# Products that nobody reads, at a block's end and beside 24 maxima

## The chip, the cores and the metric

The kernel runs on one core of a Trainium2 chip (trn2). Its time is the device time of one execution, in microseconds. It is written at the level of engines: each of the five (TensorE or PE, VectorE or DVE, ScalarE or ACT, GpSimd or POOL, SyncE or SP) has its own program, and semaphores order them.

## The reference

Two layers of a transformer over 2 batches of 1024 tokens with 256 features, in float32. Each layer is attention, an addition and layer norm, then a mixture of experts, an addition and layer norm. The change lies around the second layer's attention, which isn't causal:

```
qkv = x @ Wqkv + bqkv
q, k, v = jnp.split(qkv, [D, D + KV], axis=-1)
q = q.reshape(b, s, H, HD)                                # H = 16 heads of 16
k = jnp.tile(k.reshape(b, s, G, HD), (1, 1, H // G, 1))   # G = 4
v = jnp.tile(v.reshape(b, s, G, HD), (1, 1, H // G, 1))
scores = jnp.einsum('bqhd,bkhd->bhqk', q, k) / HD
prob = jax.nn.softmax(scores, axis=-1)
out = jnp.einsum('bhqk,bkhd->bqhd', prob, v).reshape(b, s, D)
return out @ Wout + bout
```

## The kernel before

The program is a row of blocks; at the end of a block all engines meet at a barrier. Three blocks matter here.

Block `p1` (`in_turn`) does batch 1's layer norm and its projections to queries, keys and values: 16 transposes, ACT's square root, 16 transposes back, and eight tasks of products (`("pj", m, c)`, six products of 128x512 each by `mm3`, lines 86 to 88) and transposes of the values. Beside these tasks ACT and VectorE also prepare weights for later blocks (`Projection`, `RouterWeights`). Its eight PSUM banks form a ring; a bank's reader raises `emptied`.

Block `a1` (`grouped_attention`) is the second attention. It works in 16 units (batch, four heads of each group, 512 queries), each of 16 steps. For the softmax's maximum it computes the scores twice. First with queries on the partitions: `maxima` issues two products of 48 rows by 512 columns (line 1697) into one of two slots of PSUM (`mx_ps`), and VectorE reduces the slot's 1024 columns to one negated maximum per query (line 1830, semaphore `mx_taken`). TensorE may fill a slot again when its reduction is done. The 48 rows are 16 features of queries, split in a high and a low part; heads lie at partition 0 or at 64, in turn. After the 16 maxima of a unit `turn` transposes them (line 1738), ACT copies them (line 1789), and SP sends them to the queries' tile as a 49th row (line 1668). Then keys stand on the partitions: `scores` (line 1712, one product of 49 rows), ACT's exponential (line 1811), and `values` (line 1725). The maxima run a unit and a half ahead of the scores. So 24 of them, the list `FIRST`, come ahead of the loop, with the first turn behind the 16th:

```
for u, i in FIRST:
    bank = room(ring.a_max())
    for half in range(2):
        maxima(u, i, half, bank)
    if (u, i) == (0, STEPS - 1):
        turn(-1, False, True, room(ring.a_turn(-1, False, True)))
```

The loop over units and steps follows. In each step stand, in TensorE's order, the values of an earlier step, then by turns two products of a maximum and two of scores. In unit 0 the values begin with step 4. Scores write three banks, `st_ps`, unused until then. After the attention, block `f1` has the second mixture of experts.

Of the kernel before, what the change touches and what calls it, by code (L numbers as in the profile page):

```python
# [13 lines left out]
P = 128  # L14
# [4 lines left out]
CH = 512  # L19
# [588 lines left out]
FORE = [("nf", s) for s in range(4)]  # L608
BACK = [("nb", s) for s in range(4)]
# [931 lines left out]
def grouped_attention(nc, tag, counters, queries, sides, ks, vs, z, ident, psum, rear):  # L1541
# [14 lines left out]
    with Phase(nc, tag, psum) as am:  # L1556
# [10 lines left out]
        st_ps = am.ps([P, 3, CH])  # L1567
# [112 lines left out]
        @block.tensor  # L1680
        def _(pe):
            ring = Slots()

            def room(at):
                for sem, n in at[1] or ():
                    pe.wait_ge(sem, n)
                return at[0]

            def maxima(u, i, half, bank):
                b, j, c = UNITS[u]  # L1690
                q, g = head_of(i)
                p0 = (g // 2) * HALFP
                if i == 0 and half == 0:
                    pe.wait_ge(q_in[u % QSLOT], (u // QSLOT + 1) * 192)
                    if j == 0 and c == 0:
                        pe.wait_ge(sides[b].k_in, sides[b].K_LOADS)
                m = pe.matmul(mx_ps[:, bank, half, :], qq[p0:p0 + ROWS, u % QSLOT, g % 2, q * P:(q + 1) * P],  # L1697
                              ks[b][p0:p0 + ROWS, g % 2, half * CH:(half + 1) * CH], start=True, stop=True)
                if half == 1:
                    m.then_inc(mx_ready, 1)  # L1700

            def scores(u, i, k):
                b, j, c = UNITS[u]
                n = u * 2 * STEPS + 2 * i + k
                kt, g = i // 2, (1 - i % 2) * 2 + k
                p0 = (g // 2) * HALFP
                if i == 0 and k == 0:
                    pe.wait_ge(m_in[u % QSLOT], (u // QSLOT + 1) * 64)
                if n >= 3:

                    pe.wait_ge(exp_done, n - 2)
                pe.matmul(st_ps[:, n % 3, :], ks[b][p0:p0 + ROWS + 1, g % 2, kt * P:(kt + 1) * P],  # L1712
                          qq[p0:p0 + ROWS + 1, u % QSLOT, g % 2, :], start=True, stop=True).then_inc(st_ready, 1)

            def values(n, half):
                u, kt = n // NK, n % NK
                b, j, c = UNITS[u]
                x = slice(half * CH // 2, (half + 1) * CH // 2)
                if half == 0:
                    pe.wait_ge(exp_done, (n + 1) * G1)  # L1720
                if kt == 0 and half == 0 and u >= 1:

                    pe.wait_ge(zt_done, u)
                for g in range(G1):
                    m = pe.matmul(acc_ps[g * W:(g + 1) * W, x], vs[b][:, kt, g, :], pt[:, n % SLOTS, g, x],  # L1725
                                  start=kt + half == 0, stop=kt + half == NK, tile_position=(0, g * W))
                if half == 1:
                    m.then_inc(pv_done, 1)

            def turn(u, with_z, with_m, bank):  # L1730
                if with_z:
                    pe.wait_ge(zt_done, u)
                    for q in range(NQ):
                        m = pe.transpose(mx_ps[:, bank, 0, q * P:(q + 1) * P], zt[:, q * P:(q + 1) * P], ident[:])
                    m.then_inc(z_turned, 1)
                if with_m:
                    pe.wait_ge(mx_taken, (u + 2) * STEPS)
                    pe.transpose(mx_ps[0:G1 * NQ, bank, 1, 0:P], negm[:, (u + 1) % 2, :], ident[:]).then_inc(m_turned, 1)

            for u, i in FIRST:  # L1740
                bank = room(ring.a_max())
                for half in range(2):
                    maxima(u, i, half, bank)
                if (u, i) == (0, STEPS - 1):
                    turn(-1, False, True, room(ring.a_turn(-1, False, True)))
            for u in range(LAST + 1):
                for i in range(STEPS):
                    for n, half in values_at(u, i):
                        values(n, half)
                    ahead = maxima_at(u, i)  # L1750
                    if ahead:
                        bank = room(ring.a_max())
                    for k in range(2):
                        if ahead:
                            maxima(*ahead, k, bank)
                        scores(u, i, k)
                    if i == TURN and (u > 0 or u < LAST):
                        turn(u, u > 0, u < LAST, room(ring.a_turn(u, u > 0, u < LAST)))
                    for side, t in rear_at(u, i):
                        if (side, t) == rear[0][1]:  # L1760
                            for sem, n in SPARE_FREE:
                                pe.wait_ge(sem, n)
                        side.tensor(pe, t, rear_ring)
            for n in range(LAG):
                for half in range(2):
                    values((LAST + 1) * NK - LAG + n, half)
            turn(LAST + 1, True, False, room(ring.a_turn(LAST + 1, True, False)))
# [93 lines left out]
            keep_z(LAST, ring.a_turn(LAST + 1, True, False)[0])  # L1861


def in_turn(nc, tag, counters, psum, tasks, begins=(), store=None):


    with Phase(nc, tag, psum) as ph:
        banks = ph.ps([P, 8, CH])
        ring = Ring(counters, [banks[:, k, :] for k in range(8)])
        enlist(ring, tasks)  # L1870
        block = ph.block()

        @block.sync
        def _(sp):
            for o in begins:
                if isinstance(o, (Projection, RouterWeights)):
                    o.sync(sp)
            for o in begins:
                if isinstance(o, Queries):
                    o.sync(sp)  # L1880
            if store is not None:
                store[0].store(sp, *store[1:])

        @block.gpsimd
        def _(pool):
            for o in begins:
                if isinstance(o, QKVHalf):
                    o.gpsimd(pool)

        @block.tensor  # L1890
        def _(pe):
            for side, t in tasks:
                side.tensor(pe, t, ring)

        @block.scalar
        def _(act):
            for side, t in tasks:
                side.scalar(act, t, ring)
            for o in begins:
                if isinstance(o, (Projection, RouterWeights)):  # L1900
                    o.scalar(act)

        @block.vector
        def _(dve):
            for side, t in tasks:
                side.vector(dve, t, ring)
            for o in begins:
                if isinstance(o, (Projection, RouterWeights)):
                    o.vector(dve)


def program(nc, a, out):
    with ExitStack() as stack:
# [5 lines left out]
        xh = sb("xh", [P, DT, T], F32R)  # L1919
# [5 lines left out]
        psum = stack.enter_context(nc.psum_tensor("psum", [P, 8, CH], F32))  # L1925
        rows = out.rearrange("b s d -> (b s) d")
        counters = Counters(nc, stack)
# [12 lines left out]
        def tasks(o, kinds):  # L1940
            return [(o, t) for t in kinds]

        PAUSE = [None]
        PROJECT = [("pj", 2, 0), ("pj", 2, 1), ("pj", 0, 0), ("pj", 0, 1), ("vt", 0), ("vt", 1), ("pj", 1, 0), ("pj", 1, 1)]
# [20 lines left out]
        with Phase(nc, "g") as g:  # L1965
# [16 lines left out]
            wo = Projection(g, "wo", a["wo1"], a["bo1"])  # L1982
            rw1 = RouterWeights(g, "rw1", w1, False)
            n2a = norm(g, "n2a", 0)
            with Phase(nc, "x") as x:
                wqkv = Projection(x, "wqkv", a["wqkv1"], a["bqkv1"])
# [22 lines left out]
                with Phase(nc, "s1") as s:  # L2009
                    n1b = norm(s, "n1b", 1)  # L2010
                    kv, khi, klo = (o[:].rearrange("p s n -> p (s n)") for o in (raw_gu, hi_gu, lo_gu))
                    x1 = QKVHalf(s, "x1", 1, wqkv, kv, khi, klo, xh, xl, ident, "n1b").into(qhi[1], qlo[1], ks[1], vs[1])
                    in_turn(nc, "p1", counters, psum, tasks(n1b, FORE + [("root",)] + BACK) + tasks(x1, PROJECT), (x1, wo, rw1, queries))
                    o1a = OutHalf("o1a", 0, wo, z[0], qhi[0], qlo[0], xh, xl, yT, ident, idr)
                    follows(n2a, o1a)
                    order = [TURN[0], TURN[1], GATHER[0], GATHER[1], TURN[2], TURN[3], GATHER[2], GATHER[3]]
                    rear = list(zip((1, 2, 4, 6, 8, 9, 11, 13, 15, 17, 19, 21), tasks(o1a, order) + tasks(n2a, FORE)))
                    grouped_attention(nc, "a1", counters, queries, (x0, x1), ks, vs, z, ident, psum, rear)
# [107 lines left out]
```

## Time and profile before

| | |
|---|---|
| median of 3 runs | 2160.67 us (2160.27 to 2162.22) |
| the profiled execution | 2152.04 us |
| its span | 2150.0 us |
| mean granted clock | 0.986 of full |
| TensorE busy | 2080.3 us, 97% |
| VectorE busy | 1460.8 us, 68% |
| ScalarE busy | 1221.3 us, 57% |
| GpSimd busy | 577.9 us, 27% |

The profile is of one execution, and its time isn't one of the three of the median. Durations of TensorE's products overlap, since each is recorded from its start to the end of its way through the array; how fast they follow each other is read from the distance of their starts. The granted clock is given as a part of full speed: 1.00 is 2.4 GHz, 0.50 is 1.2 GHz; a stretch with a value between holds both.

### The profile page before, as it was taken

How to read it: one execution, taken by the hardware profiler on the slowest of the kernel's cores; microseconds unless marked ns; L12 is line 12 of the kernel's file. 1: busy time of each engine (PE TensorE's matmuls, PEld its weight loads, DVE VectorE, ACT ScalarE, POOL GpSimd, SP SyncE). 2: the span in 40 equal slices, each digit the busy share in tenths (PEclk: the TensorE clock that was granted, in tenths of full speed). 3: DMA queues.
4: the chain of work that ended last, by engine and by line, in shares of the span. 5: the costliest groups of instructions: out<-in, count | busy, mean ns of one | idle time of the engine just before them, and what ended most of it. 6: DMA issues, size and time to landing. Idle time of an engine off the chain costs nothing. (4 is left out here: it accounts for less than half of the span.)

```text
span 2150.0 us, 33338 instructions
## 1 busy us (share of the span) xinstructions
PE 2080.3 (97%) x12160; PEld 1592.7 (74%) x12160; DVE 1460.8 (68%) x2761; ACT 1221.3 (57%) x2435; POOL 577.9 (27%) x679
## 2 busy tenths in 40 slices
PE   7999999999999999989999988999999899999997
PEld 6888888888788888877788873333334688778886
DVE  5666666677677666666656558999994556655555
ACT  5666666666556666554444443888887434444433
POOL 3444444444334444332222210000000112222221
PEclk9999999999999999999999996999999999999999
DMA  2000000000000000011111121101000111111111
GB/s 74 20 21 13 21 21 20 21 21 20 9 20 21 20 21 20 4 38 45 39 48 40 45 46 30 24 18 23 21 12 2 43 37 45 45 45 44 45 52 56
DMA packets 54309, 64.92 MB, mean 30 GB/s; under 512 B 9179, under 2 KB 34566, under 8 KB 54150
## 3 DMA queue, kind: packets, MB, share of 16 engines
q1 hardware_dynamic: 54150, 62.81, 10.4%
q8 instruction: 98, 1.61, 0.3%
q14 instruction: 61, 0.50, 0.1%
HBM read 52.68 MB, written 2.10 MB: 25 GB/s over the span
## 5 line engine op out<-in xcount | busy, mean ns | idle before, releaser
L862 POOL TENSOR_TENSOR a_pr<-a_pr,a_rinv 128x512 f32<-128x512 f32 (+3 forms) x384 | 312.8, 829 | 477.1 <-DVE a_rinv L1109 477.1
L86 PE MATMUL psum<-xh,g_hi_gu 128*128 128x512 f32 x928 | 377.8, 407 | 15.1 <-DVE xl L1092 8.9
L88 PE MATMUL psum<-xh,g_lo_gu 128*128 128x512 f32 x928 | 363.7, 392 | 0.0
L87 PE MATMUL psum<-xl,g_hi_gu 128*128 128x512 f32 x928 | 363.2, 391 | 0.0
L1830 DVE TENSOR_REDUCE a_negm<-psum 128x1 f32<-128x1024 f32 x256 | 309.7, 1223 | 17.5 <-PE psum L1697 16.5
L1190 POOL TENSOR_TENSOR g_lo_gu<-g_raw_gu,g_hi_gu 128x512 fp32r<-128x512 f32 x84 | 108.9, 1297 | 778.1 <-ACT g_hi_gu L1186 778.1
L1811 ACT ACTIVATE a_pt<-psum 128x512 f32<-128x512 f32 x512 | 276.4, 597 | 60.4 <-PE psum L1712 32.6
L1484 DVE TENSOR_TENSOR f_hl<-f_hid,f_hh 128x512 fp32r<-128x512 f32 x168 | 116.8, 695 | 238.4 <-ACT f_hh L1422 236.5
L1411 ACT ACTIVATE f_act_s<-psum,g_gu_bias 128x512 f32<-128x512 f32 x168 | 115.0, 685 | 277.7 <-PE psum L88 277.4
L1014 ACT ACTIVATE a_pr<-psum,a_negm 128x128 f32<-128x128 f32 (+7 forms) x256 | 190.2, 743 | 106.9 <-DVE a_negm L1099 102.9
L1021 ACT ACTIVATE a_pth<-psum 128x512 fp32r<-128x512 f32 (+3 forms) x384 | 174.9, 490 | 113.0 <-PE psum L921 110.3
L86 PEld LDWEIGHTS psum<-xh,g_hi_gu 128*128 128x128 f32 x928 | 175.0, 189 | 55.5 <-issue 13.3
L88 PEld LDWEIGHTS psum<-xh,g_lo_gu 128*128 128x128 f32 x928 | 174.7, 188 | 38.6
L1116 DVE TENSOR_TENSOR a_ptl<-psum,a_pth 128x512 fp32r<-128x512 f32 (+3 forms) x384 | 201.1, 551 | 1.4 <-ACT a_pth L1021 1.2
L1697 PE MATMUL psum<-x_ks,x_queries_qq 48*128 48x512 f32 x512 | 193.4, 468 | 7.1 <-DVE a_negm L1830 4.4
L87 PEld LDWEIGHTS psum<-xl,g_hi_gu 128*128 128x128 f32 x928 | 175.4, 189 | 31.9
L1422 ACT ACTIVATE f_hh<-f_hid 128x512 fp32r<-128x512 f32 x168 | 105.4, 627 | 157.8 <-DVE f_hid L1478 153.7
L1099 DVE CUSTOM_DVE_ANT_0 psum<-psum,a_mask 128x128 f32<-128x128 f32 (+7 forms) x256 | 191.7, 749 | 1.5 <-PE psum L88 0.2
L1712 PE MATMUL psum<-x_queries_qq,x_ks 49*128 49x512 f32 x512 | 188.5, 449 | 1.6 <-ACT a_pt L1811 0.5
L921 PE MATMUL psum<-ident,a_pr 128*128 128x128 f32 x1152 | 170.6, 275 | 9.2 <-DVE a_ptl L1116 7.0
L1697 PEld LDWEIGHTS psum<-x_ks,x_queries_qq 48*128 48x128 f32 x512 | 81.6, 197 | 113.9 <-DVE a_negm L1830 96.5
L1725 PE MATMUL psum<-a_pt,x_vs 128*32 128x256 f32 x2048 | 160.9, 392 | 0.0
(298 smaller groups left out, 4313.7 us busy)
## 6 DMA issues: line engine op xcount, KB each, us to landing
g_raw_gu<-in_gu SPq DMA_DIRECT2D x84, 256.0 KB, 2.8
f_raw_dn<-in_down SPq DMA_DIRECT2D x84, 128.0 KB, 2.0
g_raw_gu<-in_qkv SPq DMA_DIRECT2D x32, 256.0 KB, 2.8
a_wvr<-in_qkv SPq DMA_DIRECT2D x32, 128.0 KB, 2.4
a_wor<-in_o SPq DMA_DIRECT2D x32, 128.0 KB, 2.0
x_queries_qq<-x_qhi SPq DMA_DIRECT2D x128, 32.0 KB, 2.0
yT<-in_xT SPq DMA_DIRECT2D x4, 512.0 KB, 7.1
x_queries_qq<-x_qlo SPq DMA_DIRECT2D x64, 32.0 KB, 1.9
```

Of the source, the lines that this page charges most:

```text
L86: pe.matmul(out, a_hi, b_hi, start=first, stop=False)
L87: pe.matmul(out, a_hi, b_lo, start=False, stop=False)
L88: return pe.matmul(out, a_lo, b_hi, start=False, stop=last)
L862: pool.tensor_tensor(x, x, rinv[:, j:j + 1].to_broadcast([P, count * P]), ALU.mult).then_inc(p_done, 1)
L1014: act.activation(split(qt, pr[qt % NP][:, 0:n]), scored(qt), ACT.Exp, bias=negm[:, qt % NP:qt % NP + 1], scale=-1.0, accum_out=rsum[:, qt ...
L1021: act.activation(pth[c][:, rows_of(c, k0, count, qt % CQ), :], t_ps[:, n % 2, 0:count * P].rearrange("p (k q) -> p k q", q=P), ACT.Copy).t ...
L1099: dve.tensor_tensor_reduce(x, x, split(qt, mask[:, S - (qt + 1) * P:S]), -1.0, 3.0e38, ALU.add, ALU.min, negm[:, qt % NP:qt % NP + 1]).the ...
L1116: dve.tensor_tensor(ptl[c][:, p, :], t_ps[:, n % 2, 0:count * P].rearrange("p (k q) -> p k q", q=P), pth[c][:, p, :].bitcast(F32), ALU.sub ...
L1697: m = pe.matmul(mx_ps[:, bank, half, :], qq[p0:p0 + ROWS, u % QSLOT, g % 2, q * P:(q + 1) * P], ks[b][p0:p0 + ROWS, g % 2, half * CH:(half ...
L1712: pe.matmul(st_ps[:, n % 3, :], ks[b][p0:p0 + ROWS + 1, g % 2, kt * P:(kt + 1) * P], qq[p0:p0 + ROWS + 1, u % QSLOT, g % 2, :], start=True ...
L1811: act.activation(pt[:, s % SLOTS, g, :], st_ps[:, n % 3, :], ACT.Exp, scale=1.0 / HD1).then_inc(exp_done, 1)
L1830: dve.tensor_reduce(negm[:, u % 2, g * NQ + q:g * NQ + q + 1], mx_ps[:, bank, :, :], AX.XY, ALU.max, negate=True).then_inc(mx_taken, 1)
```

## The change

Two groups of products are added on TensorE. Nothing reads what they write, and no semaphore is raised by them.

At the end of `p1` ten products of 128 rows by 512 columns go to the bank that is next in the ring, after a wait for its last reader. Their operands are the projection's weights and the normalised input. Only this call of `in_turn` has the new argument.

In `a1` two products follow each of the 24 maxima of `FIRST`, ahead of the turn where there is one. They multiply a part of batch 0's keys, 128 rows, with 512 of its columns, into two banks of `st_ps`. That is 48 products.

```
@@ grouped_attention, TensorE
                 bank = room(ring.a_max())
                 for half in range(2):
                     maxima(u, i, half, bank)
+                for n in range(2):
+                    pe.matmul(st_ps[:, n, :], ks[0][:, 0, 0:P], ks[0][:, 1, 0:CH], start=True, stop=True)
                 if (u, i) == (0, STEPS - 1):
                     turn(-1, False, True, room(ring.a_turn(-1, False, True)))
@@ in_turn
-def in_turn(nc, tag, counters, psum, tasks, begins=(), store=None):
+def in_turn(nc, tag, counters, psum, tasks, begins=(), store=None, unread=None):
@@ in_turn, TensorE
             for side, t in tasks:
                 side.tensor(pe, t, ring)
+            if unread is not None:
+                bank = ring.banks[len(ring.at) % len(ring.banks)]
+                pe.wait_ge(ring.emptied, ring.last(bank))
+                for n in range(10):
+                    pe.matmul(bank, unread[0], unread[1], start=True, stop=True)
@@ program
-                    in_turn(nc, "p1", counters, psum, tasks(n1b, FORE + [("root",)] + BACK) + tasks(x1, PROJECT), (x1, wo, rw1, queries))
+                    in_turn(nc, "p1", counters, psum, tasks(n1b, FORE + [("root",)] + BACK) + tasks(x1, PROJECT), (x1, wo, rw1, queries),
+                            unread=(wqkv.wh[:, 0, 0:P], xh[:, 0, 0:CH]))
```

TensorE's order at the border between `p1` and `a1`; `x_wqkv` are the projection's weights, `xh` the input, `x_ks` the keys, L1680 the branch into `a1`:

```order
 L88 MATMUL psum<-xh,x_wqkv_wl 128x512
+L1900 MATMUL psum<-xh,x_wqkv_wh 128x512 x10
 L54 UNCONDITIONAL_BRANCH
 L1680 UNCONDITIONAL_BRANCH
-L1697 MATMUL psum<-x_ks,x_queries_qq 128x512 x32
+L1697 MATMUL psum<-x_ks,x_queries_qq 128x512 x2
+L1745 MATMUL psum<-x_ks 128x512 x2
+L1697 MATMUL psum<-x_ks,x_queries_qq 128x512 x2
+L1745 MATMUL psum<-x_ks 128x512 x2
```

Before, the last product of the projections was followed by the barrier and then by 32 products of 16 maxima; now ten unread ones stand ahead of the barrier, and a pair of them behind each maximum. The same engine at the first turn (L1738), where the 16th maximum's pair stands ahead of it:

```order
+L1697 MATMUL psum<-x_ks,x_queries_qq 128x512 x2
+L1745 MATMUL psum<-x_ks 128x512 x2
 L1738 MATMUL psum<-ident,a_negm 16x128
-L1697 MATMUL psum<-x_ks,x_queries_qq 128x512 x17
+L1697 MATMUL psum<-x_ks,x_queries_qq 128x512 x2
+L1745 MATMUL psum<-x_ks 128x512 x2
```

The turn stays behind the 16th maximum. The 17 products behind it are those of eight maxima and the first of the loop's step 0; the eight now have a pair each, and the loop has none.

## Rows read from the trace of the kernel before

**Rows 1.** The page: its head, and the granted clock in 40 slices.

```profile
span 2150.0 us, 33338 instructions
...
PEclk9999999999999999999999996999999999999999
```

**Rows 2.** Windows: stretch, length, busy time (instructions) of each engine, clock, DMA.

```profile
1289.28:1291.95 2.67, 0.00 (x0) 0.03 (x1) 1.56 (x4) 1.62 (x4) 0.00 (x0) 1.00 0.00 0
1291.95:1293.74 1.79, 0.73 (x4) 0.30 (x4) 1.04 (x1) 0.00 (x0) 0.00 (x0) 1.00 0.40 60
1293.74:1312.79 19.05, 16.45 (x28) 6.95 (x28) 17.82 (x16) 0.00 (x0) 0.00 (x0) 0.50 0.31 56
...
1323.38:1331.28 7.90, 7.72 (x36) 3.17 (x36) 6.60 (x6) 5.43 (x10) 0.00 (x0) 0.50 0.04 9
```

**Rows 3.** Timeline from the projections' end: start, length, engine, line, tiles.

```profile
1288.65 0.39 PE L87 MATMUL psum<-xl,x_wqkv_wh 128*128 128x512 f32 x1
1288.88 0.40 PE L88 MATMUL psum<-xh,x_wqkv_wl 128*128 128x512 f32 x1
...
1291.30 0.18 DVE L285 TENSOR_TENSOR g_rw_gwl<-g_rw_gw,g_rw_gwh 128x32 fp32r<-128x32 f32 x1
...
1291.95 0.73 PE L1697 MATMUL psum<-x_ks,x_queries_qq 48*128 48x512 f32 x4 [2.68 <-PEq L54]
...
1292.70 2.35 DVE L1830 TENSOR_REDUCE a_negm<-psum 128x1 f32<-128x1024 f32 x2 [1.22 <-PE psum L1697]
...
1293.98 2.35 PE L1697 MATMUL psum<-x_ks,x_queries_qq 48*128 48x512 f32 x4 [1.29 <-DVE a_negm L1830]
```

**Rows 4.** Groups of instructions on VectorE, 1292.6 to 1324.6 us.

```profile
L1830 DVE TENSOR_REDUCE a_negm<-psum 128x1 f32<-128x1024 f32 x24 | 28.3, 1220 | 4.7 <-PE psum L1697 4.7
```

**Rows 5.** Timeline around the first turn.

```profile
1310.43 2.36 DVE L1830 TENSOR_REDUCE a_negm<-psum 128x1 f32<-128x1024 f32 x2 [0.17 <-PE psum L1697]
...
1312.94 0.37 PE L1738 MATMUL psum<-ident,a_negm 128*16 128x128 f32 x1 [1.41 <-DVE a_negm L1830]
...
1314.50 2.36 DVE L1830 TENSOR_REDUCE a_negm<-psum 128x1 f32<-128x1024 f32 x2 [1.70 <-PE psum L1697]
```

**Rows 6.** Timeline of TensorE in the loop's first steps.

```profile
1323.38 0.79 PE L1697 MATMUL psum<-x_ks,x_queries_qq 48*128 48x512 f32 x1 [0.18 <-DVE a_negm L1830]
...
1323.97 0.62 PE L1697 MATMUL psum<-x_ks,x_queries_qq 48*128 48x512 f32 x1
...
1324.51 0.79 PE L1697 MATMUL psum<-x_ks,x_queries_qq 48*128 48x512 f32 x1
...
1331.35 0.49 PE L1697 MATMUL psum<-x_ks,x_queries_qq 48*128 48x512 f32 x1
...
1331.69 0.39 PE L1697 MATMUL psum<-x_ks,x_queries_qq 48*128 48x512 f32 x1
...
1332.01 0.64 PE L1725 MATMUL psum<-a_pt,x_vs 128*32 128x256 f32 x8
1332.58 0.49 PE L1697 MATMUL psum<-x_ks,x_queries_qq 48*128 48x512 f32 x1
```

**Rows 7.** Timeline of TensorE at the second turn, at the upper clock.

```profile
1337.09 0.28 PE L1738 MATMUL psum<-ident,a_negm 128*16 128x128 f32 x1
1337.29 0.64 PE L1725 MATMUL psum<-a_pt,x_vs 128*32 128x256 f32 x8
```

**Rows 8.** Windows over two other stretches in which TensorE had pauses.

```profile
1268.00:1273.90 5.90, 2.18 (x18) 1.73 (x16) 2.83 (x13) 4.43 (x7) 2.85 (x3) 1.00 0.27 63
17.10:20.50 3.40, 1.92 (x13) 1.44 (x12) 1.94 (x8) 2.73 (x8) 1.69 (x3) 1.00 0.00 0
```

**Rows 9.** Timeline of TensorE at the lower clock, products over 128 rows.

```profile
543.98 0.63 PE L88 MATMUL psum<-a_pth,a_vl 128*128 128x512 f32 x1
544.40 0.63 PE L86 MATMUL psum<-a_pth,a_vh 128*128 128x512 f32 x1
```

**Rows 10.** SP's queue: the issues that send the maxima's row.

```profile
1313.64 2.52 SPq L1668 DMA_DIRECT2D x_queries_qq<-a_mrow  x4
```

## The prediction

> **What bounds the kernel now.** I read the page's head first, then the slices, then stretches around the place of the change, and last the rows of single instructions. The span is 2150.0 us, and TensorE's granted clock stands at its upper level (2.4 GHz) in nearly all slices; one shows a six [rows 1]. That slice is where both edits lie. The windows cut it apart [rows 2]. TensorE does nothing for 2.67 us at the end of batch 1's projections, four products and 0.73 us of work follow in the next 1.79 us, and from 1293.74 us on the clock is at 0.50, the lower level (1.2 GHz), though TensorE is then busy for 16.45 of 19.05 us. It is still at 0.50 when the attention's loop begins at 1323.38 and until 1331.28.
>
> Ahead of the loop only VectorE and TensorE work, in a chain through two PSUM slots: two products fill a slot (L1697), one reduction empties it (L1830). The 24 reductions kept VectorE busy for 28.3 us and it idled 4.7 us, all of it until TensorE's products came [rows 4]. A pair of reductions takes 2.35 us with 1.22 us for one, so they can start 1.13 us apart [rows 3, 4]. From 1292.70 to the end of the 16th at 1312.79 are eight pairs, 2.53 us from pair to pair [rows 3, 5]. So a reduction has a period of 1.27 us at the lower clock, where VectorE alone would need 1.13. This stage is a plain chain; what it gives back moves everything behind it forward.
>
> **The terms.** I measure from the first reduction (1292.70) to the point where the loop's values of step 6 start (1332.01 [rows 6]), since from 1331.28 the clock is up and the loop has its steady step: 1331.35 to 1332.58 is 1.23 us [rows 6], before as after. I place the changed kernel on the profiled execution's own time line.
>
> *The ten products ahead of the block's end.* Products over all 128 rows start 0.23 us apart [rows 3]. Ten start at 1289.11 and end at 1288.88 + 10 x 0.23 + 0.39 = about 1291.6. VectorE's last instruction of that block ends at 1291.30 + 0.18 = 1291.48 [rows 3], and the block ends for all engines together. They cost 0.15 us beyond their cover (ACT's and VectorE's weight preparation); without that cover it would be 2.3 us. The bank that they write was emptied long ago (its reader is the rounding of the first projection). Bounds: 0 and 0.5 us, since the barrier's own handling is not shown with TensorE last.
>
> *The 48 products beside the maxima.* If the clock holds, what is TensorE's period for two maxima and two unread products? Maxima follow each other 0.34 and then 0.32 us apart at the upper clock (1331.35, 1331.69, 1332.01); at the lower one 0.59 and 0.54 (1323.38, 1323.97, 1324.51) [rows 6]. Products over all rows need 0.23 [rows 3]. I take a change between the two kinds at 0.32, as from a maximum to the values. So 0.34 + 0.32 + 0.23 + 0.32 = 1.2 us. VectorE's floor is 1.13. TensorE is thus the bound by a little, at 1.20. For a reduction to be ready after its slot is free, 1.23 + 0.05 + 0.75 us (1291.95 to 1292.70 [rows 3]) must fit into two periods, 2.03 in 2.40: it does. Only the two maxima of a slot stand ahead of its reduction, so the unread pair delays the next slot alone.
>
> The rule against 1.20 is about the weights' load. First the row: products over all rows keep 0.23 us [rows 3], too short for a load that stands by itself ahead of each. The Trainium skill, TensorE: Matmul & The Clock Gate, "The mechanism", says that a load of weights overlaps a running product only when their row groups differ; by it the second unread product would start 0.32 us after the first as well, the period would be 1.29, and the result that of the third case below.
>
> *Sum.* First reduction at 1292.85. Fifteen periods of 1.20: the 16th starts at 1310.85 and ends at 1312.08. Then the turn of the maxima: 0.15 us until L1738 starts, as 1312.79 to 1312.94 [rows 5]; 0.20 until the next product [rows 7]; 0.75 until its reduction: 1313.18, where before had 1314.50 [rows 5]. The unread pair stands ahead of the turn's wait and is done by then. Seven periods more: the 24th reduction at 1321.58. The loop's first maximum is issued behind the last unread pair at about 1322.03 (before: 1323.38 [rows 6]). Steps 0 to 3 have no values; at the upper clock TensorE needs 0.65 for such a step, so VectorE's 1.13 rules: the 25th reduction starts at 1322.03 + 0.75 = 1322.78, the 26th at 1323.91, and the maximum of step 3 may go when the 26th has ended, 1323.91 + 1.23 + 0.05 = 1325.19. Step 4's values start 0.65 later at 1325.84, take 0.57 (1332.01 to 1332.58 [rows 6]), step 5's at 1327.06, step 6's at 1328.28. Before: 1332.01. Gain 3.7 us: 1.35 stand at the loop's first maximum (shorter periods and a turn shorter by 0.6, less the 0.15 of the ten products), and 2.4 come from the loop's first six steps, which no longer run at the lower clock.
>
> Is anything else late then? The row of maxima is sent by SP from 1313.64 for 2.52 us [rows 10] and is needed at 1323.38, 7 us after its last issue. Both move forward, by 0.7 and by 1.35 us; a slack of over 6 us stays.
>
> Against the profiled execution (2152.04 us, 2.04 beyond its span) this gives 2148.3. The median of the runs shown, 2160.67, is 8.6 us above it; I take the gain as the same there: **2157.0 us**.
>
> **The rivals.**
> 1. *VectorE bounds the filled stage.* If the change between kinds costs less than 0.32, TensorE's period falls under 1.13, and 22 periods are 0.07 shorter: gain 3.7 + 1.5 = 5.2 us, 2155.4. For it: loads are hidden between products over all rows [rows 3]. Against it: they are not between maxima (0.32 and not 0.23).
> 2. *The clock holds, but products queue.* With 0.32 for each change and for the second unread product the period is 1.29: gain 3.7 - 22 x 0.09 = 1.7 us, 2158.9. The same time comes out when the barrier waits for the ten products in full, or when the clock falls for a few of the maxima. Here belongs also that the later fall (after this attention) and the rise of the clock meet the program at other places; it can add or take some 1.5 us. I give this group, down to no gain, its own chance.
> 3. *The clock falls all the same* (slower). Place: the idle time ahead of the turn. TensorE has finished its pair 1.4 us before L1738 may start. Then a maximum with its unread pair costs 0.59 + 0.54 + 0.54 + 0.42 = 2.09 us (the last from 543.98 to 544.40, products over all rows at half clock [rows 9]), against 1.27 before. Eight maxima after the turn lose 8 x 0.82 = 6.6, less the 0.7 won until then: 2166.6. Lost from the very start it would be 22 x 0.82, 18 us: 2178.7. A maximum at the lower clock costs 0.89 over one at the upper, so it decides from 4 of the 24 maxima on. For it: from 17.10 to 20.50 us TensorE was busy for 1.92 of 3.40 us, with the clock at 1.00, and it fell right after [rows 8]. Against it: from 1268.00 to 1273.90 it was busy for 2.18 of 5.90 us and the clock stayed [rows 8], and the filled stage keeps TensorE busy nearly throughout. With 16.45 of 19.05 us in products over 48 rows the clock did not come back [rows 2]; the unread ones go over all 128 rows, as does the work of the projections, in which the clock is high. Whether they hold it in this mixture no row of before shows; I choose that they do.
> The Trainium skill, TensorE: Matmul & The Clock Gate, "A second HAM failure mode: psum-queue depth-cycling", says that short idle times between groups of products, while PSUM banks are cycled, can make the clock swing; here it would be this third case, and the trace so far leaves it open.
> 4. *Nothing changes*: the clock is low as before and the products fit. Excluded at 2.09 over 1.27; it would be case 3.
>
> **From this to the numbers.** The clock holds with period 1.2: 0.48. Rival 1: 0.22. Rival 2 with gains of 0 to 3: 0.19. Rival 3: 0.11. What a measurement of this kernel can tell from no change is about 0.2%, 4.3 us. Rival 1 passes that nearly always, the likeliest case in about three of ten, by the later clock's places or a shorter period; so faster 0.34. Slower by as much is rival 3 and little else: 0.11. Within it: 0.55. The range reaches from rival 1 with half a microsecond more (2154.8) to no gain at all (2160.8), and leaves out rival 3 and the extremes. The likeliest case's own range is 2155.8 to 2158.4.
>
> **What the profile would show.** The slice with the six turns into a nine; the windows from 1293.74 on have a clock of 1.00 up to the loop and through its first steps. L1900 x10 starts 0.23 us apart and the first maximum comes at 1291.95 to 1292.4. L1745 x48, the first of a pair about 0.32 after the maximum. Reductions start 1.20 apart: a first-to-16th distance of 18.0 us (17.0 in rival 1, 19.4 in rival 2, 18.9 before, at 2.53 per pair). The idle time ahead of the 17th reduction falls from 1.70 to 1.1 us. Step 6's values come 35.4 us after the first reduction, not 39.3. Busy time of VectorE and ACT stays; TensorE's count grows by 58. I am wrong if the clock falls between L1900 and the loop, if the pairs of L1745 take over 0.64 us at the upper clock, or if the time returns later, at the first wait for queries or in the stages behind the attention.

## The result and the profile after

The change made the kernel slower: the median of nine executions is 2169.79 us (2162.86 to 2171.11), against 2161.07 us for nine of before; the ratio is 1.0039, with a 95% interval of 1.0023 to 1.0056. The two sets of times do not overlap: the slowest of before took 2162.22 us. A ratio, here and below, compares all executions of two kernels and not their medians, and leaves out one execution in the study, 2178.46 us of a version with fewer products, since it lies over 1.5% above the fastest of its kernel. The profiled execution took 2169.98 us with a span of 2167.8.

The page's head and the slices of the clock of the changed kernel, which answer to [rows 1]:

```profile
span 2167.8 us, 33454 instructions
...
PEclk9999999999999999999999996899999999999999
```

Each digit is the granted clock of a fortieth of the span, in tenths of full speed. The six is still there and has an eight behind it. The windows of the changed kernel show where the clock was low, as [rows 2] did for before:

```profile
1290.49:1312.82 22.33, 21.58 (x66) 9.70 (x67) 19.60 (x16) 0.07 (x1) 0.00 (x0) 1.00 0.30 53
1312.82:1330.92 18.10, 18.10 (x34) 7.69 (x34) 9.62 (x8) 1.48 (x2) 0.00 (x0) 0.50 0.10 23
1330.92:1367.43 36.51, 36.25 (x198) 13.05 (x201) 21.78 (x19) 19.58 (x37) 0.00 (x0) 0.50 0.03 7
1367.43:1390.00 22.57, 22.32 (x214) 8.87 (x205) 20.85 (x20) 19.23 (x37) 0.00 (x0) 1.00 0.07 16
```

The clock is at 1.00 through the block's end and the first sixteen maxima. It falls at 1312.82, 0.37 us after the first turn's product has started, and stays at 0.50 for 54.6 us: through the other eight maxima, in which TensorE is busy for all of 18.10 us, and through the loop's first 36.5 us. TensorE's timeline of the changed kernel shows what the added products cost at either clock:

```profile
1287.55 2.49 PE L1900 MATMUL psum<-xh,x_wqkv_wh 128*128 128x512 f32 x10
1290.49 0.70 PE L1697 MATMUL psum<-x_ks,x_queries_qq 48*128 48x512 f32 x2 [0.45 <-PEq L54]
1291.12 0.73 PE L1745 MATMUL psum<-x_ks 128*128 128x512 f32 x2
1291.78 0.73 PE L1697 MATMUL psum<-x_ks,x_queries_qq 48*128 48x512 f32 x2
1292.44 0.73 PE L1745 MATMUL psum<-x_ks 128*128 128x512 f32 x2
1293.10 0.73 PE L1697 MATMUL psum<-x_ks,x_queries_qq 48*128 48x512 f32 x2
...
1310.97 0.73 PE L1745 MATMUL psum<-x_ks 128*128 128x512 f32 x2
1312.45 0.27 PE L1738 MATMUL psum<-ident,a_negm 128*16 128x128 f32 x1 [0.75 <-DVE a_negm L1832]
...
1314.82 1.22 PE L1697 MATMUL psum<-x_ks,x_queries_qq 48*128 48x512 f32 x2
1315.96 1.22 PE L1745 MATMUL psum<-x_ks 128*128 128x512 f32 x2
1317.12 1.22 PE L1697 MATMUL psum<-x_ks,x_queries_qq 48*128 48x512 f32 x2
```

Read the starts. From one maximum to the next are 1.32 us at the upper clock (1291.78 to 1293.10), 0.32 to 0.34 for each of the four products, where before took 1.27 at the lower one. At the lower clock it is 2.30 us (1314.82 to 1317.12). A pair is one row here: the second product starts 0.34 us behind the first and takes 0.39, together the 0.73 shown. Ahead of the turn (L1738) TensorE sat idle for 0.75 us.

Two lengths are needed below, that of the maxima's part and that of the loop's first unit. They are read between three starts: the first reduction, the first product of scores (L1712), the first copy of the values (`a_zt`, the end of the loop's first unit). The copy of before (its first profile), and that of the changed kernel:

```profile
1348.72 0.60 ACT L1796 ACTIVATE a_zt<-psum 128x512 f32<-128x512 f32 x1 [0.17 <-PE psum L1725]
```

```profile
1368.01 0.60 ACT L1798 ACTIVATE a_zt<-psum 128x512 f32<-128x512 f32 x1 [0.88 <-PE psum L1725]
```

For the changed kernel the three starts are 1291.2, 1330.9 and 1368.0: 39.7 us of maxima and 37.1 us of the first unit. For before, first profile, they were 1292.7, 1323.4 and 1348.7: 30.7 and 25.3. The two parts grew by 20.8 us, while the spans differ by 17.8; so the whole loss against that profile lies in them, and 3.0 were won elsewhere. Half of these 3.0 stand ahead of the first reduction (1291.2 against 1292.7). The 17.8 us are also twice the 8.7 between the medians, which is the first riddle.

### The profile page after: what moved, and what is told of

It reads as the page before. It is cut to its first block and busy times, and to the rows that moved or that the text cites. A ratio compares the mean times of both kernels' runs of the same rounds, so it can differ in the third digit from the quotient of the medians.

```text
span 2167.8 us, 33454 instructions
## 1 busy us (share of the span) xinstructions
PE 2104.4 (97%) x12218; PEld 1602.8 (74%) x12218; DVE 1461.1 (67%) x2761; ACT 1220.1 (56%) x2435; POOL 576.8 (27%) x679
## 5 line engine op out<-in xcount | busy, mean ns | idle before, releaser
L1832 DVE TENSOR_REDUCE a_negm<-psum 128x1 f32<-128x1024 f32 x256 | 310.9, 1224 | 37.1 <-PE psum L1697 34.7
L1712 PE MATMUL psum<-x_queries_qq,x_ks 49*128 49x512 f32 x512 | 194.7, 462 | 1.6 <-ACT a_pt L1813 0.5
L1725 PE MATMUL psum<-a_pt,x_vs 128*32 128x256 f32 x2048 | 166.7, 405 | 0.0
```

Of the source, the lines that this page charges most:

```text
L1832: dve.tensor_reduce(negm[:, u % 2, g * NQ + q:g * NQ + q + 1], mx_ps[:, bank, :, :], AX.XY, ALU.max, negate=True).then_inc(mx_taken, 1)
```

## The experiments

Two theories were formed on these rows. Theory A: the pairs hold the clock only where no idle time of TensorE comes between them; once it has fallen they cost 1.03 us each over before. The rest depends on when the clock comes back in the loop, which differs between executions, in before too: its nine executions were one of 2147.88 and eight of 2159.78 to 2162.22, and the profile that the prediction rests on (2152.04) does not stand for the usual execution. Theory B: before is quick in the loop, and the change alone makes it slow there.

**The kernel before once more.** No edit.

> The kernel before, unchanged, to see a second profile of it. Theory A (the added pairs are paid at the lower clock, and the loop starts at the lower clock in the usual execution of before as well): the span is about 2159, some 9 us over the first profile's 2150.0, and the granted clock stays at 0.50 well beyond 1331 us, into the loop's second unit, with loop steps of 2.16 us instead of 1.23. Theory B (before is quick in the loop, the change alone makes its first steps slow): the clock is up again at about 1331 us, the span is 2150 to 2152, and the gap to the median is something the profile doesn't show.

Measured: 2160.49 us, span 2158.3. Its windows over the loop's beginning, and TensorE's timeline in it:

```profile
1321.64:1353.60 31.96, 31.78 (x169) 10.93 (x169) 19.99 (x17) 17.50 (x33) 0.00 (x0) 0.50 0.01 3
1353.60:1370.00 16.40, 16.24 (x157) 6.60 (x153) 15.24 (x15) 13.67 (x26) 0.00 (x0) 1.00 0.12 27
```

```profile
1326.38 1.08 PE L1725 MATMUL psum<-a_pt,x_vs 128*32 128x256 f32 x8
...
1328.54 1.08 PE L1725 MATMUL psum<-a_pt,x_vs 128*32 128x256 f32 x8
...
1330.70 1.08 PE L1725 MATMUL psum<-a_pt,x_vs 128*32 128x256 f32 x8
```

This is theory A's case. The maxima took 30.7 us as in the first profile (1290.9 to 1321.6), but the loop ran at the lower clock until 1353.6, with steps of 2.16 us (1326.38, 1328.54, 1330.70) where the upper clock has 1.23. Its first unit took 35.1 us and not 25.3. Against this profile the changed kernel's maxima are 9.0 us longer and its first unit 2.0 us, and the spans differ by 9.5, near the 8.7 of the medians: this is the riddle's answer. In 23 further executions of before, 8 lie at 2148.3 to 2154.6 and 15 at 2159.4 to 2165.6, and their mean clock is 0.985 to 0.988 and 0.977 to 0.982. The prediction's profile was of the first group, here about a third of the executions, and its median of the second.

**Each part alone.** Only the ten products (without the pairs), and only the pairs (without the ten):

```
-                for n in range(2):
-                    pe.matmul(st_ps[:, n, :], ks[0][:, 0, 0:P], ks[0][:, 1, 0:CH], start=True, stop=True)
```

> Only the ten products at the end of batch 1's projections. Theory A: the maxima alone don't hold the clock, it falls a few us later than before, the loop is entered at 0.50; time as before within 3 us. Theory B (the ten products hold or lose something by themselves): 5 us or more off before, either way.

```
-                            unread=(wqkv.wh[:, 0, 0:P], xh[:, 0, 0:CH]))
```

> Only the 48 products beside the maxima. Theory A: the pause of 2.7 us at the block's end lets the clock fall in the first maxima; all 24 maxima then cost 2.3 us each instead of 1.27, about 20 to 24 us over before (2181 to 2185). Rival: the clock stays up through the block's end in some executions, then the time is that of the change, 2163 to 2171.

The ten alone gave a median of 2151.15 us in ten executions (2149.4 to 2163.81), ratio 0.9989 (0.9965 to 1.0013): no difference that can be told. Six executions fell at 2149 to 2151 and four at 2162 to 2164, the two groups of before. The profiled one took 2151.01 us. Its clock fell at 1292.5, within the first maxima, which took 30.7 us together, as before; the first unit took 25.3 us, as in the first profile of before.

The pairs alone gave 2180.70 us (2177.74 to 2184.32, four executions), ratio 1.0107 (1.0076 to 1.0139). VectorE's timeline in it:

```profile
1292.75 2.58 DVE L1832 TENSOR_REDUCE a_negm<-psum 128x1 f32<-128x1024 f32 x2 [1.21 <-PE psum L1697]
1296.40 1.23 DVE L1832 TENSOR_REDUCE a_negm<-psum 128x1 f32<-128x1024 f32 x1 [1.07 <-PE psum L1697]
1298.70 1.23 DVE L1832 TENSOR_REDUCE a_negm<-psum 128x1 f32<-128x1024 f32 x1 [1.07 <-PE psum L1697]
```

The clock fell with the second maximum, as behind the same pause of 2.7 us in before, and the later reductions are 2.30 us apart with 1.07 or 1.08 idle each, but for the one behind the turn. The maxima took 53.6 us. So neither the ten products nor the pairs alone kept the clock up beyond the first maxima; in the changed kernel, with both, it stayed up. And with the pairs still running at the lower clock and TensorE busy for 52.25 of 52.51 us, the clock did not come back before the loop.

**The sixteen maxima alone.** Pairs beside the maxima ahead of the turn, none behind it:

```
-                for n in range(2):
+                for n in range(2 if u == 0 else 0):
```

> The change with pairs beside the first sixteen maxima only. Theory A (the 8 to 9 us lost are the eight pairs at the lower clock behind the turn): the clock falls at the turn, the eight maxima behind it take 1.27 us each, the time is that of before within 2 us, both its usual value and its spread. Theory B (the loss comes from the first sixteen or from the ten products): 2166 to 2170 as the change.

Measured: 2162.92 us (2159.95 to 2172.67, ten executions), ratio 1.0035 (1.0011 to 1.0058). In the profile the maxima took 31.4 us, against 39.7 with all pairs and 30.7 before: 8.3 us of the change's 9.0 in this part are the eight pairs behind the turn, as theory A has it. The clock fell at 1314.1, again 0.4 us after the turn's product had started, with 0.74 us idle ahead of it. The time as a whole does not bear theory A out: the profiled execution was at 2159.95, with a first unit of 33.3 us, but three of ten were at 2172.6 to 2172.7, where before has none, and none of the ten lies in before's lower group (13 of 35), so the spread isn't that of before. The interval lies above 1. No slow execution of this version was profiled; why its loop is late more often stays open.

**The turn filled.** Four more unread products behind the sixteenth pair:

```
+                if (u, i) == (0, STEPS - 1):
+                    for n in range(4):
+                        pe.matmul(st_ps[:, n % 2, :], ks[0][:, 0, 0:P], ks[0][:, 1, 0:CH], start=True, stop=True)
                 if (u, i) == (0, STEPS - 1):
                     turn(-1, False, True, room(ring.a_turn(-1, False, True)))
```

> The change plus four more unread products between the sixteenth pair and the first turn, where the changed kernel's TensorE idles 0.75 us and the clock falls. Theory A: the clock stays at 1.00 through the turn, the eight maxima behind it take 1.32 us each and not 2.3, and the loop runs its first steps at 1.23; the turn itself is 0.5 us late. About 2150, some 10 us under before and 19 under the change. Theory B (the pairs themselves don't hold the clock for as long as this, or the loop's slow start has another cause): 2165 to 2171 as the change.

Measured: 2163.88 us (2150.39 to 2172.37, twelve executions), ratio 1.0024 (1.0001 to 1.0047). Half of theory A came out: the turn, but not the loop and not the time. TensorE's timeline at the turn and in the loop's first steps:

```profile
1311.51 1.09 PE L1748 MATMUL psum<-x_ks 128*128 128x512 f32 x4
1312.44 0.27 PE L1738 MATMUL psum<-ident,a_negm 128*16 128x128 f32 x1
1312.64 0.73 PE L1697 MATMUL psum<-x_ks,x_queries_qq 48*128 48x512 f32 x2
...
1325.27 0.49 PE L1697 MATMUL psum<-x_ks,x_queries_qq 48*128 48x512 f32 x1 [0.36 <-DVE a_negm L1835]
...
1326.41 0.79 PE L1697 MATMUL psum<-x_ks,x_queries_qq 48*128 48x512 f32 x1 [0.40 <-DVE a_negm L1835]
```

The clock held through the turn and all 24 maxima, 32.0 us of them. The idle time ahead of L1738 is gone and the turn is not late at all (1312.44 as against 1312.45). But in the loop's steps 0 to 3 no values stand, TensorE has 0.65 us of work over 48 and 49 rows for VectorE's 1.13, and at 1326.4 the clock fell (a product of 0.49 us becomes one of 0.79). From the loop's start to there TensorE was busy for 2.44 of 3.18 us. The first unit then took 36.9 us. My expectation had overlooked that these steps leave TensorE idle as the maxima without their pairs do. The profile is one of twelve executions that differ widely: that at 2150.39 us has a mean clock of 0.996, as if it had never fallen here, and the two above 2170 have 0.983 and 0.984, as the change has. None of these was profiled.

**The loop filled as well.** One more product behind the scores of these steps:

```
+                    if u == 0 and i < 4:
+                        for n in range(1):
+                            pe.matmul(acc_ps[:, :], ks[0][:, 0, 0:P], ks[0][:, 1, 0:CH], start=True, stop=True)
                     if i == TURN and (u > 0 or u < LAST):
```

> The change, the four products ahead of the turn, and one more unread product behind the scores of each of the loop's steps 0 to 3 of unit 0, where no values stand yet and the clock fell at 1326 us in the run before this one. Theory A (each thin place between the projections and the values must be filled, and then the clock holds): clock 1.00 from 1290 us to the end of the attention, loop steps of 1.23 us from the start, 2148 to 2152 in every execution, about 10 us under the usual 2160 of before. Theory B (the pairs only postpone a fall that comes anyway): a fall within 30 us of the loop's start, 2158 to 2166.

Measured: 2150.54 us (2148.37 to 2153.11, twelve executions), ratio 0.9965 (0.9950 to 0.9981). This is faster than before and than the change (whose fastest took 2162.86), and the spread is gone: before had 35 executions from 2148.92 to 2165.18 on the same chip. Its windows:

```profile
1290.00:1325.05 35.05, 34.60 (x109) 16.17 (x107) 30.16 (x27) 2.72 (x6) 0.00 (x0) 1.00 0.23 43
1325.05:1329.41 4.36, 4.36 (x22) 1.94 (x21) 4.26 (x5) 3.81 (x8) 0.00 (x0) 1.00 0.10 23
1329.41:1348.60 19.19, 18.73 (x188) 7.02 (x189) 17.99 (x15) 15.87 (x32) 0.00 (x0) 1.00 0.04 8
```

The clock is at 1.00 throughout these windows; the maxima took 32.0 us and the first unit 23.5. All twelve executions have a mean clock of 0.993 to 0.997.

**Fewer products beside the maxima.** As the version before this one, with one beside the even and two beside the odd ones:

```
-                for n in range(2):
+                for n in range(1 + i % 2):
```

> As the kernel with the loop filled, with one unread product beside the even maxima and two beside the odd ones. Theory A, by the measured 0.33 us for each of a maximum's and a pair's products at the upper clock: a period of 1.16 us instead of 1.32, 24 of them 3.8 us less, 2145 to 2149 if the clock holds with fewer products. If it doesn't: a fall within the maxima, maxima of 2.0 us behind it, 2160 to 2172.

Measured: 2148.63 us in the median of ten, ratio 0.9983 (0.9947 to 1.0019). In the profile the maxima took 29.2 us, 2.8 less than with pairs, and the clock held. Seven executions are at 2144.88 to 2149.73 with a mean clock of 0.994 to 0.997, the fastest of the study among them; three are at 2171.51 to 2178.46 with 0.979 to 0.982. Such a mean clock fits an early fall, but none of the three was profiled. The version is not shown to be better than the pairs, and its time is far less steady.

**Only in the loop, spaced.** The kernel before and two products behind the scores of steps 0 to 3, while the clock is low:

```
+                    if u == 0 and i < 4:
+                        for n in range(2):
+                            pe.matmul(acc_ps[:, :], ks[0][:, 0, 0:P], ks[0][:, 1, 0:CH], start=True, stop=True)
```

> The kernel before with nothing but two unread products behind the scores of steps 0 to 3 of unit 0, in the loop, while the clock is low. Theory A (most of what before loses is the loop at the lower clock, of a length that differs from one execution to the next): the steps 0 to 3 get 0.8 us longer, the clock rises with them or right behind, and nearly all executions lie at 2149 to 2154, where before has 2148 to 2166. Rival (the loop's slow stretch is something that eight products can't end): 2160 to 2166, before plus 3 us.

Measured: 2162.66 us (2155.99 to 2176.26, twelve executions), ratio 1.0025 (1.0004 to 1.0046). Theory A's expectation was wrong here. The steps became 2.30 us long, TensorE was never idle in them, and the clock came back only at 1355.4. The first unit took 37.6 us. The stretch from the first values to the clock's return:

```profile
1332.61:1355.40 22.79, 22.79 (x130) 7.29 (x129) 11.90 (x11) 10.99 (x21) 0.00 (x0) 0.50 0.00 1
```

TensorE is busy for all of it.

**Only in the loop, in a row.** The kernel before with sixteen products in a row ahead of the loop, and one in each of steps 0 to 3:

```
+            for n in range(16):
+                pe.matmul(acc_ps[:, :], ks[0][:, 0, 0:P], ks[0][:, 1, 0:CH], start=True, stop=True)
             for u in range(LAST + 1):
                 for i in range(STEPS):
```

> The kernel before with sixteen unread products in a row right ahead of the loop, and one behind the scores of steps 0 to 3 of unit 0; none at the block's end, none beside the maxima. Theory A (a row of products over 128 rows brings the clock back, which the spaced pairs of the loop-only run did not, and the loop's thin steps hold it with one each): the maxima at the lower clock as before, 30.7 us to the loop plus 3.7 to 6.9 us for the row, the clock up ahead of the loop or within it, first unit of the loop in 23.5 us as in the filled kernel, 2151 to 2156 in every execution. Rival (once low ahead of this loop, the clock stays low until deep in it whatever stands there): 2164 to 2170.

Measured: 2154.48 us (2153.61 to 2156.34, twelve executions), ratio 0.9986 (0.9969 to 1.0003). TensorE's timeline:

```profile
1321.37 2.35 PE L1697 MATMUL psum<-x_ks,x_queries_qq 48*128 48x512 f32 x4 [0.18 <-DVE a_negm L1835]
1323.65 6.08 PE L1747 MATMUL psum<-x_ks 128*128 128x512 f32 x16
1329.66 0.50 PE L1697 MATMUL psum<-x_ks,x_queries_qq 48*128 48x512 f32 x1
```

The row took 6.0 us and the clock came back within it, at 1328.3, which is 4.6 us after its start: the loop's first product has 0.50 us and not 0.79. The first unit took 23.5 us. All twelve executions lie within 2.7 us of each other. Their median is 4.0 us above the mean of before's lower group (six of 17 on this chip, 2148.70 to 2152.50) and 5 to 10 us below its upper group (2159.65 to 2164.60). The median moved by 5.4 us, but the interval still touches 1, so a gain is not shown. What separates before's two groups, by its two profiles, is the loop's first unit (25.3 and 35.1 us, where the spans differ by 8.3), and this version, whose clock is up in that unit, has one group only. It also shows that the maxima can be left at the lower clock at little cost: 30.7 us in before, 32.0 with pairs at the upper one. The row and the four single products were run only together; what the row does alone is not known.

## Why the prediction was wrong

**What bounds the kernel** held: the stage is a chain of two engines at the lower clock, and what it loses is added to the end.

**The ten products** were rightly sized. They take 2.49 us, and the first maximum came 1290.49 - 1287.55 = 2.94 us behind their start; in before it came at 1291.95, 2.84 behind the place where they would have started (1289.11). So they cost 0.1 us, where I had 0.15.

**The period of 1.20 us** was mis-sized: 1.32 was measured. I had the second unread product at 0.23 behind the first, as in products over all rows in a row. In a run this holds (ten in 2.49 us, four in 1.09), but the second of a pair between maxima comes at 0.34. That is nearly the period of rival 2, 1.29. The Trainium skill, TensorE: Matmul & The Clock Gate, "The mechanism", lets a load of weights overlap a running product only when their row groups differ. In this mixture the trace agrees in the time that it gives (0.34 us for the second of a pair); in a run of the same products it does not, since these start 0.23 us apart. So why the second of a pair is late is not shown. With 1.32 the pairs gain nothing at all in the first sixteen maxima: VectorE was served every 1.27 us at the lower clock.

**The step that failed** is "whether they hold it in this mixture no row of before shows; I choose that they do". They hold it beside the first sixteen maxima, but the clock fell right behind the turn's idle time, which the sum had passed over as harmless; that is rival 3, at the place that it names. With that idle time filled, the clock held there in the profile of that version. The idle time was 0.75 us, and not the 1.4 of the prediction, and this was enough. Rival 3's price was too low by a tenth: 2.30 us a maximum and not 2.09, since the products of the mixture start 0.56 to 0.59 us apart at the lower clock. Eight times the difference of 2.30 and 1.27 is 8.2 us, sixteen times that of 1.32 and 1.27 is 0.8, together the 9.0 that the maxima's part grew by. Rival 3 said 2166.6 us, from 5.9 lost in the maxima, and 2169.79 came, with 9.0 lost there. The chance of 0.11 was too small: the prediction had a row of a fall with TensorE busy for 1.92 of 3.40 us [rows 8], and none that showed the clock held in this mixture.

**"I take the gain as the same there"** failed too, and no rival stood for it. I read the loop from an execution in which the clock came back at 1331.28 and compared with a median in which it comes back some 22 us later. The hint was on the table, 2152.04 against 2160.27 to 2162.22, three agreeing executions with the profiled one outside. In the changed kernel the clock came back late in the loop as well, 36.5 us after its start. Had the clock held as forecast, the gain against the usual execution would have been of some 10 us, as with the loop filled, not 3.7.

**The loop's steps 0 to 3** I costed at VectorE's 1.13 with the clock up. With the turn filled it did not stay up there. Filling one thin place shows the next: block's end, maxima, turn, first steps. SP sent the maxima's row from 1313.04 for 2.52 us, long before the loop's start at 1330.92, so this slack never mattered, as forecast.

## What to carry to other kernels

Products that only keep the clock have to cover every place with idle time up to the stage that pays for it. Here each of the four versions that had pairs and left a gap was slower than before (2162.9 to 2180.7 us, each interval above 1). In their profiles the loop's first unit still ran mostly at the lower clock, and each pair behind a gap cost 1.03 us over a maximum without one. Ask first what the stage would win: here the maxima themselves ran as fast at the lower clock as at the upper one with their pairs, and what could be won was in the loop behind them. A single row of sixteen products just ahead of it, with one more in each of its first four steps, got the clock up there as well (2154.5 us, against 2150.5 for the fully filled kernel; the first isn't told from before by its interval). And when the profiled execution lies outside the timed ones, find out what differs in it, by the mean clock or a second profile, before a sum is made on it.

## What the runs showed of the hardware

A busy TensorE is not one that gets its clock back. In the eight pairs behind the turn it was busy for 18.10 of 18.10 us at the lower clock, in the loop at 2.16 us a step for 36.25 of 36.51, and the clock stayed; in sixteen products over all rows in a row it came back within 6.0 us. In twelve executions with this row the times lie within 2.7 us, so this return does not look like chance. Maxima over 48 rows, by themselves or in turn with products over 128, were never seen to bring the clock back here, not in 52.5 us. In the loop it did come back, 7.9 us after the loop's start in one execution of before and 32.0 in another of the same program; what in the loop lets it rise I did not settle.

Nor does a fall need a long pause. It came right behind 0.75 us of idle time at the turn, in the change and in the version without pairs behind the turn, and, in the version with the turn filled, in the loop's first steps with two idle times of 0.36 and 0.40 us.
